# Where the values product stands in a round of attention, and three smaller moves

## The reference

```python
xn = _layernorm(x)
x = x + L0_attn(xn) + L0_ffn(xn)     # L0: decaying scan over time, gelu MLP; ternary-weight MLP with 2 hidden products
xn = _layernorm(x)
x = x + L1_attn(xn) + L1_ffn(xn)
```

```python
rms = sqrt(mean(o * o, -1) + EPS)
o = o / rms * g_norm_w * g * sigmoid(g)
return o.reshape(B, L, H * dv) @ Wo
```

```python
scores = einsum('bqhd,bkhd->bhqk', q, k) * scale
probs = softmax(scores, -1)
attn = einsum('bhqk,bkhd->bqhd', probs, v) @ Wo + bo
x = layer_norm(src + attn)
# every token goes to expert floor(router(x)) mod 4: relu(x @ W1[e] + b1[e]) @ W2[e] + b2[e]
return layer_norm(x + ff_out)
```

## Time and profile before

| | us |
|---|---|
| median of 3 runs | 2738.59 (2737.5 to 2741.57) |
| the profiled execution | 2737.27 |
| its span, first to last instruction | 2735.4 |
| layer 0 (to about 970) | 970 |
| attention, rounds with scores (1145.2 to 2532.6) | 1387 |
| experts (about 2568 to 2735) | 167 |
| PE busy | 2427.5 (89%) |
| DVE busy | 1931.2 (71%) |
| ACT busy | 1343.0 (49%) |
| POOL busy | 593.8 (22%) |
| mean granted TensorE clock | 0.954 of full speed |

### The profile page before, as it was taken

How to read it: one execution, slowest core, us unless ns; L and a number is a source line. 1 busy time by engine, 2 the same in 40 slices (tenths; PEclk the granted TensorE clock), 3 DMA queues, 4 the chain that set the end, 5 groups by cost and what they waited for, 6 DMA issues and landing times. The chain is left out here.

```text
span 2735.4 us, 45149 instructions
## 1 busy us (share of the span) xinstructions
PE 2427.5 (89%) x14582; PEld 1679.8 (61%) x14582; DVE 1931.2 (71%) x3706; ACT 1343.0 (49%) x1926; POOL 593.8 (22%) x630
## 2 busy tenths in 40 slices
PE   3899999999999857899989998899989999999596
PEld 2788888888888745555555555555455555554385
DVE  3788888888888613667767777777767777772375
ACT  1444444444444312366566656656565656555242
POOL 0021112111211100111312222222212231211276
PEclk9999999999999978999999999999999999999898
DMA  4443432243223133423343323432342333301472
GB/s 151 125 123 116 126 99 75 75 131 93 75 75 109 43 137 93 120 86 86 103 126 96 100 93 115 119 100 83 102 135 85 93 106 91 90 24 32 142 229 96
DMA packets 195550, 280.31 MB, mean 102 GB/s; under 512 B 21672, under 2 KB 151161, under 8 KB 186880
## 3 DMA queue, kind: packets, MB, share of 16 engines
q1 hardware_dynamic: 189952, 266.47, 32.8%
q0 software_dynamic: 5504, 12.63, 1.3%
HBM read 148.65 MB, written 131.91 MB: 103 GB/s over the span
## 5 line engine op out<-in xcount | busy, mean ns | idle before, releaser
L1598 DVE TENSOR_REDUCE c_row_max<-b_psum 128x2 f32<-128x1024 f32 x512 | 624.8, 1220 | 305.9 <-PE b_psum L1308 301.5
L1445 ACT ACTIVATE c_prob<-b_psum 128x1024 f32<-128x1024 f32 x512 | 525.5, 1026 | 401.7 <-PE b_psum L1326 394.1
L1326 PE MATMUL b_psum<-c_cq,c_ck 25*128 25x512 f32 x1024 | 260.2, 504 | 76.6 <-ACT c_prob L1445 72.6
L1308 PE MATMUL b_psum<-c_bk,c_bq 24*128 24x512 f32 x1024 | 262.1, 507 | 47.6 <-DVE c_row_max L1598 34.3
L1336 PE MATMUL b_psum<-c_prob,c_v_aug 128*32 128x512 f32 x2048 | 292.4, 645 | 0.1
L1326 PEld LDWEIGHTS b_psum<-c_cq,c_ck 25*128 25x128 f32 x1024 | 96.2, 185 | 247.5 <-ACT c_prob L1445 152.2
L354 PE MATMUL a_psum<-a_yT_hi,a_w_hi 128*128 128x512 f32 x512 | 205.6, 402 | 9.3 <-issue 5.9
L354 PE MATMUL a_psum<-a_yT_hi,a_w_lo 128*128 128x512 f32 x512 | 203.2, 397 | 0.0
L354 PE MATMUL a_psum<-a_yT_lo,a_w_hi 128*128 128x512 f32 x512 | 203.0, 396 | 0.0
L518 DVE TENSOR_TENSOR_SCAN a_st_sb<-a_decay,a_kv_sb 128x512 f32<-128x512 f32 x128 | 156.8, 1225 | 4.4
L460 ACT ACTIVATE a_g<-a_psum,a_cols 128x512 f32<-128x512 f32 x64 | 44.1, 690 | 235.5 <-PE a_psum L354 235.5
(11 more groups left out here) (298 smaller groups left out, 5452.2 us busy)
## 6 DMA issues: line engine op xcount, KB each, us to landing
sorted_scratch<-a_pad SPq DMA_DIRECT2D x16, 2184.5 KB, 14.2
g_scratch<-a_g_hi SPq DMA_DIRECT2D x16, 1024.0 KB, 4.0
g_scratch<-a_g_lo SPq DMA_DIRECT2D x16, 1024.0 KB, 7.1
c_g_hi<-g_scratch SPq DMA_DIRECT2D x16, 1024.0 KB, 6.6
c_g_lo<-g_scratch SPq DMA_DIRECT2D x16, 1024.0 KB, 8.6
stack_scratch<-c_qk_hi SPq DMA_DIRECT2D x256, 64.0 KB, 1.6
d_wt<-expert_scratch SPq DMA_DIRECT2D x19, 834.0 KB
c_bq<-stack_scratch SPq DMA_DIRECT2D x128, 96.0 KB
```

Source lines behind the costliest of these rows:

```text
L1308: mm = nc.tensor.matmul(psum[:, MAX + x, :], bq[r, j, cut(t)], bk[r, j, :], start=True, stop=True)
L1326: mm = nc.tensor.matmul(psum[:, SCORE + x, :], ck[r, j, cut(kb)], cq[r, j, :], start=True, stop=True)
L1445: nc.scalar.activation(prob[:, i % 4, :, :], psum[:, SCORE:SCORE + 2, :], ACT.Exp, scale=DH1 ** -0.5).then_inc(S["exp"], 1)
L1598: nc.vector.tensor_reduce(row_max[:, t, at:at + 3:2], psum[:, MAX:MAX + 2, :], AX.X, ALU.max).then_inc(S["row_max"], 1)
```

## The change

It does four things. In odd pairs from 3 on (but for 23), pv stands between score and max, instead of behind max. The second and third quarters of w3 stand in pairs 24 and 26 instead of 25 and 27, so that they are in pairs without a pv. The squares of `osquare` and the sum `O2` stand in pair 25 instead of 23 and 24, and `O3` in 27 instead of 25. In the last stage the root of the last group stands ahead of the scatters of the one before, as it does in all other groups. And the twelve small transfers of the expert tables all stand behind the last chunk.

```diff
-                            if n >= len(prep_chunks) - len(table_parts) // 2:
-                                at = 2 * (n - len(prep_chunks) + len(table_parts) // 2)
-                                for d, plain in table_parts[at:at + 2]:
+                            if n == len(prep_chunks) - 1:
+                                for d, plain in table_parts:
                                     sp.dma_start(d, plain).then_inc(S["table_out"], 16)
...
-W3_AT = (23, 25, 27, 30)
+W3_AT = (23, 24, 26, 30)
...
-    put(23, "A1", "osquare", 0)
-    put(23, "A1", "osquare", 1)
     put(23, "A1", "gate")
-    put(24, "A1", "O2")
-    put(25, "A1", "O3")
+    put(25, "A1", "osquare", 0)
+    put(25, "A1", "osquare", 1)
+    put(25, "A1", "O2")
+    put(27, "A1", "O3")
...
     for p in range(PAIRS):
-        order += [("C", "score", p), ("B", "max", p)]
+        order.append(("C", "score", p))
         if p >= 3 and p % 2 and p != 23:
             order.append(("C", "pv", (p - 3) // 2))
+        order.append(("B", "max", p))
...
             for k in range(GROUPS):
-                if k + 2 < GROUPS:
+                if k + 1 < GROUPS:
                     root(k + 1)
...
-                if k + 2 == GROUPS:
-                    root(k + 1)
```

## The result

The changed kernel takes 2856.75 us (median of 4 runs, 2851.32 to 2866.63) against 2740.08 for the kernel before in the same series: ratio 1.0429 [1.0403, 1.0455], slower, where 2838 was forecast. The profiled execution took 2851.32 us, its span is 2849.5.

What follows compares the result with a forecast made beforehand. TensorE was taken to set the attention stage: 15 rounds x (4.4 + 0.7 + 1.7) = +102 us, last root -2.1, tables 0, on 2737.3 gives 2837.2; with 1.3 for the median, 2838 us, range 2775 to 2885.

Steps and rivals of the forecast that it cites:

- The price of pv between S and M: Odd pairs: values product between scores and maxima products costs TensorE 0.63 us more, less hidden waits; +4.4 us a round.
- the 1.19 us from pv to a narrow product: TensorE, odd pairs: a narrow product starts 1.19 us after the values product, against 0.99 for a full-height one.
- less than 1 us: Sign in odd pairs: maxima starting under 1 us behind the values product would show the first term wrong.
- The credits of pairs 5 and 6: Pair 5 costs 0, since the maxima product of pair 6 waits 0.93 us for VectorE's row maximum anyway.
- Pair 15: Moving the values product between scores and maxima in this pair costs +0.34 us at full clock.
- Pairs 23 to 30: Moved quarters and squares: old exponential waits go, new ones for VectorE and POOL come; +0.7 us a round against 20.88.
- The walk: Step-by-step new order from the scores of pair 23 to those of pair 31: 21.6 us at full clock.
- The clock: Behind the new waits, at least one half-clock stretch falls on TensorE work: +1.7 us a round, bounds 0 and 3.4.
- The last root: Last stage: POOL's root ahead of four scatters removes its 2.11 us wait; -2.1 us, bounds -2.1 and 0.
- The tables: Twelve small transfers behind the last chunk, ahead of the next input load: 0 taken, bounds -3 to +5 us once.
- Rival 4: Faster: maxima behind the values product share the array as behind scores, so the move is free; 2706 us, chance 0.07.
- Rival 2: Two half-clock stretches a round, both on the path: +25, 2864 us; chance 0.14.

Runs made afterwards that it cites:

- same row groups: Kernel before, in its order, but in pairs 24 to 31 the maxima products use the same TensorE row groups as their pair's scores; 2782.28 us.
- pv between alone: Kernel before with only the values product put between scores and maxima in the odd pairs; 2883.52 us.
- the quarters alone: Kernel before with only the quarters of w3 moved to pairs 24 and 26; 2733.46 us.

## Why the prediction was right, and where it was not

The sign and the engine were right, and the size came near: +102 - 2 was forecast, 114 came. Two terms were mis-sized, one too high and one too low, so that the size is partly luck.

**The price of pv between S and M.** Forecast 0.63 us in each odd pair, measured 0.42, from the start of pair 3 to that of pair 4. The step that failed is the 1.19 us from pv to a narrow product. That was no cost of TensorE, but a wait for an exponential, whose end the second row follows by 0.06 us. ScalarE there, and then TensorE in the kernel before in a pair where nothing else is due, which shows the true spacing, and which I had not read:

```profile
2476.38 1.02 ACT L1445 ACTIVATE c_prob<-b_psum 128x1024 f32<-128x1024 f32 x1 [0.99 <-PE b_psum L1326]
```

```profile
1679.09 1.06 PE L1336 MATMUL b_psum<-c_prob,c_v_aug 128*32 128x512 f32 x8
1680.09 0.49 PE L1326 MATMUL b_psum<-c_cq,c_ck 25*128 25x512 f32 x2
```

From pv to S 1.00 us, as to a full-height product; the prediction had named less than 1 us as the sign that this term is wrong, and it came out right at that border. With 1.00, the sum over pairs 3 to 22 would have been 3.8 - 8 x 0.21 = 2.1 us (eight pairs carry the term there); 2.0 was measured. The credits of pairs 5 and 6 (+0.29 and -0.30) and of 21 and 22 (+0.26 and -0.27) held, and pair 11 costs nothing, as it must with 1.00. Pair 15 was off: +0.13 by the corrected sum, -0.11 measured.

The rule of the Trainium skill that a change of the tiling mode drains TensorE (TensorEngine Tiling (Array Packing), Key Properties) doesn't show where I had read it, as an extra 0.20 us from pv to the narrow products: pv to a full-height product, which is a change of form too, takes 0.99. But the rule isn't refuted. In the run with the same row groups S and M follow each other without a change of form and take 0.67 us; parted by pv they take 0.43 each, 0.86. So of the 0.43 us that M adds, 0.24 are its pass and 0.19 come with the parting, which agrees with the rule in direction; no run prices a drain by itself. Its other half, that tiles work in parallel, is what the change gave up: S and M together take 0.43 us, apart 0.86.

**Pairs 23 to 30.** The walk had waits of 1.4, 1.4, 2.6 and 0.8; 1.09, 1.09, 2.46 and none came. The three places that matter were right. The walk was 21.6 us at full clock and 23.3 with the clock; S 23 to S 31 takes 24.3. Its waits were 1.6 us too long in sum, its three pv (25, 27, 29) by 0.6, and its clock too short.

**The clock.** Forecast 1.7 us in a round; the clock takes 6.8 in each steady round (3.4 in most before). The step that failed is the length of a stretch: I priced one pv and one quarter on work behind a wait, as if the wait alone set it. What the runs show in its place: parting S and M lengthens it, behind the same waits (pv between alone, 13.7) and with nothing between them (same row groups, 3.4 to 13.7). Like for like (the 20.88 us of before hold 3.4 of clock) the forecast was 15 x (1.7 - 3.4) = -25 for the clock and +127 for queue and waits; of the 122.6 us measured, 59 are clock by the table and 64 the rest. In the steady rounds the errors nearly cancel, by luck: 6.9 us each, 6.8 forecast.

**The rounds 13 and 14.** I multiplied one round by 15. In the last two no products with h2 and w3 stand between the narrow ones; there half clock appears in pairs 8 to 22 as well (pair 14 of round 13 takes 5.75 us instead of 4.02), and they cost +35.4 instead of +13.6. These 21.8 us are the whole excess of the rounds over the +102 (20.6).

**The last root:** -2.1 forecast; the 2.11 gap is gone, and the stages behind the rounds take 2.5 less in the run that changes only root and tables. In the changed kernel it is 6.9; of the other 4.4 us, 1.3 are in the last round, and for the rest I have no cause. One trace of a kernel says little here: from the end of the 15 rounds to the end of the span it takes 256.7 to 262.2 us in the seven kernels with the old root (262.2 in the kernel before, the longest) and 254.0 to 259.6 in the seven with the early one, 2.3 less on the mean. **The tables:** 0 forecast; layer 0 ends 3.9 us earlier on the mean in the seven kernels with the late tables, and the rounds begin some 5 earlier, outside my bounds. Twelve issues in a row don't make the input late; why the start is earlier I didn't try.

**The rivals.** Rival 4 needed pv to M to the next product under 1.2 us; it is 1.43. That the move isn't free is shown by each of the runs with it. Rival 2, which had the clock worse than the forecast, was nearest in time (2864); but it had two stretches where one long one came, and without the last two rounds the time would have been nearer the forecast.

What stays open: why parted narrow products go with longer half clock at all, and why a stretch behind the same wait is short in one round and over 20 us long in another, with the same instructions. No run here changes that alone.

## What to carry to other kernels

Two narrow pairs of products on complementary row groups are worth more side by side than the 0.42 us that parting them costs in the queue: in this kernel both things that were put between them lost time, even the work that filled a wait. Read a spacing as the cost of an instruction only where no other wait could have set it, and check the rounds at the end of a pipeline by themselves. A wait removed is a gain only with what is late next moved along: the quarters alone gave 0.2%, with one more instruction moved by one pair (and root and tables) 2.2%.

## What the runs showed of the hardware that I had not expected

- Half clock follows waits of 0.56 to 1.2 us here, in some rounds and not in others, and can last while TensorE is busy (0.50 granted over 23.10 us, 21.91 of them busy and 1.20 a wait near its start). The long stretches came where narrow products stood in series among the others.
- The same instructions behind the same wait give stretches of different length from round to round: 0.53 over 29 us and 0.84 over 21.2 in one execution; rounds of 88 and 92.2 in another, whose kernel scatters (2724.73 to 2776.83 us in ten runs).
- From the values product (128 rows x 32 columns) to a narrow pair on two row groups takes 1.00 us, as to a full-height product (0.99 in the earlier trace rows). Two narrow pairs on the same row groups that follow each other take 0.67 us, two that are parted by another form 0.86.
